# Leaving o out of the second half's sum and gates in an LSTM step, and forming it in later gaps

## The reference

```python
def step(carry, xw_t):                       # L0, 512 steps in sequence
    prev_h, prev_c = carry
    a = xw_t + prev_h @ Wh                   # Wh is 512 x 2048, order i, f, o, g
    i = sigmoid(a[:, :H]); f = sigmoid(a[:, H:2*H]); o = sigmoid(a[:, 2*H:3*H])
    g = tanh(a[:, 3*H:])
    next_c = f * prev_c + i * g
    next_h = o * tanh(next_c)
    return (next_h, next_c), next_h
x = x + lstm(x, cond, Wx, Wh, b)
x = x + ssm(x, cond, conv_b, Wp, bp, Ws, bs, A_log, dt_log, Wo, bo)   # convolution, projections, a linear scan
```

## Time and profile before

| | us |
|---|---|
| median of 3 runs | 1920.33 (1919.08 to 1920.81) |
| the profiled execution | 1920.7 |
| its span | 1918.8 |
| one step in mid-run | 3.57 (DVE's line 951 of half 0 at 1000.30 and 1003.87) |

### The profile page before, as it was taken

The page is one execution under the profiler, slowest core; times in us unless marked ns, Lnnn a source line. Parts: engine busy times, 40 slices in busy tenths (PEclk is TensorE's granted clock), DMA queues, the critical chain, the costliest instruction groups (busy, mean ns, idle before and its releaser), DMA issues.

```text
span 1918.8 us, 123325 instructions
## 1 busy us (share of the span) xinstructions
PE 1814.8 (95%) x52714; PEld 1422.2 (74%) x52714; DVE 1389.9 (72%) x6917; ACT 1015.4 (53%) x4055; POOL 340.0 (18%) x1544
## 2 busy tenths in 40 slices
PE   5888999999999999999999999999999999999976
PEld 3666777777777777777777777777777777777865
DVE  8676667777677776777777677777777777767675
ACT  5555455555555555555555545556555555545442
POOL 1111111111111111111111111111111111111110
PEclk9999999999999999999999999999999999999998
DMA  6111111111111211111111111211111111211100
GB/s 236 51 45 37 48 53 37 51 56 43 54 49 41 64 41 55 48 47 56 47 56 40 53 54 39 62 45 51 53 52 48 45 56 40 72 39 48 47 15 24
DMA packets 112668, 100.81 MB, mean 53 GB/s; under 512 B 20353, under 2 KB 86453, under 8 KB 111094
## 3 DMA queue, kind: packets, MB, share of 16 engines
q1 hardware_dynamic: 111704, 90.79, 15.5%
q10 hardware_dynamic: 416, 2.13, 0.3%
HBM read 50.90 MB, written 41.94 MB: 48 GB/s over the span
## 4 chain that ended last, share of the span: by engine, by line
PE 78%; DVE 10%; ACT 5%; issue 3%; POOL 2%; DMA 1%; SPq 0%; ACTq 0%; POOLq 0%; DVEq 0%
PE recA L546 28%; PE recB L553 23%; PE pw L505 12%; PE pbc L623 10%; DVE tr L937 4%; ACT act L819 3%; POOL h L472 2%; DVE hz L968 2%; DVE pre L943 2%; DVE prod L951 1%; ACT tc L829 1%; PE pw L489 1%; PE po L643 1%; PE pu L596 1%; DMA wpk<-in_L_cond_Wh_dram 1%
## 5 line engine op out<-in xcount | busy, mean ns | idle before, releaser
L819 ACT ACTIVATE act<-pre 128x64 f32<-128x64 f32 x1024 | 262.7, 257 | 858.3 <-DVE pre L946 841.0
L546 PE MATMUL recA<-whi,hz 128*16 128x256 f16 x8176 | 516.7, 275 | 74.8 <-DVE hz L968 63.1
L553 PE MATMUL recB<-whi,hz 128*32 128x128 f16 x16352 | 578.8, 219 | 1.1 <-issue 1.1
L553 PE MATMUL recB<-wlo,hz 128*32 128x128 f16 x16352 | 578.6, 219 | 0.0
L546 PE MATMUL recA<-wlo,hz 128*16 128x256 f16 x8176 | 513.3, 273 | 0.0
L553 PEld LDWEIGHTS recB<-whi,hz 128*32 128x32 f16 x16352 | 438.5, 97 | 11.3 <-issue 1.6
L553 PEld LDWEIGHTS recB<-wlo,hz 128*32 128x32 f16 x16352 | 438.3, 97 | 2.5
L546 PEld LDWEIGHTS recA<-whi,hz 128*16 128x16 f16 x8176 | 200.2, 88 | 304.1 <-DVE hz L968 281.3
L937 DVE STREAM_TRANSPOSE tr<-recA 128x256 f32<-128x256 f32 x512 | 229.9, 449 | 198.3 <-PE recA L546 196.3
L623 PE MATMUL pbc<-yt,wpk 128*128 128x256 f32 (+5 forms) x1120 | 329.5, 400 | 0.0
L472 POOL TENSOR_TENSOR h<-osc,tc 128x16 f32<-128x16 f32 x1024 | 228.1, 223 | 467.2 <-ACT tc L829 467.2
(11 more groups left out here) (164 smaller groups left out, 1993.0 us busy)
## 6 DMA issues: line engine op xcount, KB each, us to landing
xw_rows<-xs SPq DMA_DIRECT2D x128, 256.0 KB, 2.3
seed<-xw_rows SPq DMA_DIRECT2D x1008, 32.0 KB, 2.0
xn<-in_x_dram SPq DMA_DIRECT2D x32, 256.0 KB
out_dram<-ot SPq DMA_DIRECT2D x32, 256.0 KB, 3.1
seed<-in_L_cond_Wh_dram ACTq DMA_DIRECT2D x2, 1024.0 KB, 6.8
wpk<-in_L_cond_Wh_dram SPq DMA_DIRECT2D x2, 1024.0 KB, 12.0
wlo<-in_L_cond_Wx_dram SPq DMA_DIRECT2D x2, 1024.0 KB, 13.3
xs<-in_L_cond_Wx_dram SPq DMA_DIRECT2D x1, 1024.0 KB, 9.5
```

The costliest lines, as they stand in the source:

```text
L546: ins = pe.matmul(rec[0][32 * j:32 * j + 2 * NB, 0:256].rearrange("p (c f) -> p c f", c=2), h[:, 2 * NB:4 * NB], w[:, k, :, :].rearrange(" ...
L553: ins = pe.matmul(rec[1][32 * j:32 * j + 32, 0:128], h[:, 2 * NB * (1 - c):2 * NB * (1 - c) + 32], w[:, k, 4 * (2 + c) + j, :], start=Fals ...
L819: act_eng.activation(act[q][:, 0:G, :].rearrange("p g n -> p (g n)"), pre[q][:, :, :, :].rearrange("p g c b -> p (g c b)"), ACT.Tanh, scal ...
```

## The change

Half 1 no longer takes o through the same add and the same tanh as the other gates. Its transpose reads the two 64 column halves of recB in reverse order, so that the blocks lie as o, g, i, f in tr[1], pre[1] and act[1]. `add` and `gates` of half 1 work on rows 1 to 3 (48 elements). o's own sum is a new DVE instruction `add_o` between half 0's cell and half 1's product. o's tanh is a new ACT instruction `gate_o` in the place of `opened`. osc[1] = (o + 1) SC is formed on POOL instead of ACT, between POOL's two products. `product` reads its operands at the new places. Half 0 is as it was.

```diff
+        ifgate, gc = (act[0][:, 0:2, :], act[1][:, 2:4, :]), (act[0][:, 3:5, :], act[1][:, 1:5:3, :])
@@ gpsimd
                 pool.tensor_scalar(osc[0][:, :], act[0][:, 2, :], 1.0, SC, ALU.add, ALU.mult).then_inc(s_os[0], 1)
                 for q in range(2):
+                    if q:
+                        pool.wait_ge(s_tgo, t + 1)
+                        pool.tensor_scalar(osc[1][:, :], act[1][:, 0, :], 1.0, SC, ALU.add, ALU.mult).then_inc(s_os[1], 1)
                     pool.wait_ge(s_tc[q], t + 1)
                     pool.wait_ge(s_os[q], t + 1)
@@ scalar
             def gates(t, q):
                 act_eng.wait_ge(s_add[q], t + 1)
-                act_eng.activation(act[q][:, 0:G, :].rearrange("p g n -> p (g n)"),
-                                   pre[q][:, :, :, :].rearrange("p g c b -> p (g c b)"), ACT.Tanh, scale=gain).then_inc(s_tg[q], 1)
-
-            def opened(t):
-
-                act_eng.wait_ge(s_tg[1], t + 1)
-                act_eng.activation(osc[1][:, :], act[1][:, 2, :], ACT.Copy, bias=SC, scale=SC).then_inc(s_os[1], 1)
+                act_eng.activation(act[q][:, q:G, :].rearrange("p g n -> p (g n)"),
+                                   pre[q][:, q:G, :, :].rearrange("p g c b -> p (g c b)"), ACT.Tanh, scale=gain).then_inc(s_tg[q], 1)
+
+            def gate_o(t):
+                act_eng.wait_ge(s_addo, t + 1)
+                act_eng.activation(act[1][:, 0, :], pre[1][:, 0, :, :].rearrange("p c b -> p (c b)"), ACT.Tanh,
+                                   scale=gain).then_inc(s_tgo, 1)
@@ scalar, order of a step
                     tanh_c(t, 0)
-                    opened(t)
+                    gate_o(t)
@@ vector
             def open_(t, q):
                 dve.wait_ge(s_rec[q], t + 1)
-                order = ("p c g z b -> p (c g z b)", "p g c z b -> p (g c z b)")[q]
-                dve.transpose(tr[q][:, :, :, :, :].rearrange(order), rec[q][:, 0:WIDTH[q]]).then_inc(s_tr[q], 1)
+                if q:
+                    dve.transpose(tr[1][:, :, :, :, :].rearrange("p g c z b -> p (g c z b)"),
+                                  rec[1][:, 0:128].rearrange("p (a f) -> p a f", a=2)[:, ::-1, :]).then_inc(s_tr[1], 1)
+                else:
+                    dve.transpose(tr[0][:, :, :, :, :].rearrange("p c g z b -> p (c g z b)"), rec[0][:, 0:256]).then_inc(s_tr[0], 1)
             def add(t, q):
                 dve.wait_ge(s_tr[q], t + 1)
                 if q:
-                    dve.tensor_tensor(pre[1][:, :, :, :], tr[1][:, :, :, 0, :],
-                                      tr[1][:, :, :, 1, :], ALU.add).then_inc(s_add[1], 1)
+                    dve.tensor_tensor(pre[1][:, 1:G, :, :], tr[1][:, 1:G, :, 0, :],
+                                      tr[1][:, 1:G, :, 1, :], ALU.add).then_inc(s_add[1], 1)
+            def add_o(t):
+                dve.tensor_tensor(pre[1][:, 0, :, :], tr[1][:, 0, :, 0, :], tr[1][:, 0, :, 1, :],
+                                  ALU.add).then_inc(s_addo, 1)
             def product(t, q):
                 dve.wait_ge(s_tg[q], t + 1)
-                dve.scalar_tensor_tensor(prod[q][:, :, :], act[q][:, 0:2, :], 1.0, act[q][:, 3:5, :],
+                dve.scalar_tensor_tensor(prod[q][:, :, :], ifgate[q], 1.0, gc[q],
                                          ALU.add, ALU.mult).then_inc(s_prod[q], 1)
@@ vector, order of a step
                     add(t, 1)
                     cell(t, 0)
+                    add_o(t)
                     product(t, 1)
```

More of the change, by code:

```diff
@@ L140, in lstm_ssm_kernel @@
         s_tg = [sem(f"s_tg{q}") for q in range(2)]
+        s_addo, s_tgo = sem("s_addo"), sem("s_tgo")
         s_tc = [sem(f"s_tc{q}") for q in range(2)]
```

## The result

The changed kernel takes 1943.4 us (median of 4 runs, 1940.5 to 1948.24) against 1919.7 us (4 runs, 1918.29 to 1920.81) for the kernel before on the same chip: a ratio of 1.0125, 95% interval 1.0111 to 1.0139. It is slower by 24 us where 14 us less was forecast. The profiled execution took 1948.2 us with a span of 1946.3.

What follows compares the result with a forecast made beforehand. The prediction took half 1's chain in the recurrence loop to bound the kernel, not TensorE. 15 + 17 = 32 ns a step gave 14.3 us, from 1920.33 to 1906.0; forecast 1902 to 1911 (70%), range 1901 to 1917.

Steps and rivals of the forecast that it cites:

- What bounds the step: Recurrence loop ending in `low`: half 1's chain sets the step by about 0.02 us, half 0 right behind.
- The add: Half 1's add on DVE, 64 to 48 elements: 15 ns less, on the path of both chains.
- The gates: Half 1's gates on ScalarE, 64 to 48 elements: 17 ns less for half 1, about 12 ns for half 0.
- The sum: Whole run: 436 x 0.032 + 17 x 0.018 = 14.3 us gained.
- The reversed read: recB's transpose on DVE: price 0 taken, slack 0.01; as a slower rival up to 0.12 us longer, 1956, 5%.
- o's sum and tanh in their gaps: `add_o` in DVE's idle 0.24 us and `gate_o` in the copy's place on ScalarE: price 0 each.
- o + 1 on GpSimd: Third GpSimd instruction, 0.20 us, between the halves' products: price 0, slack 0.08 at the lower bound, none at the upper.
- my own upper bound: A 0.08 gap on GpSimd before o + 1, ending 1005.19, just when half 1's `high` wants it.
- The sign that I had named for being wrong: On DVE, `high` of half 1 waiting for GpSimd instead of its tanh would show the prediction wrong.
- GpSimd is late: Rival: gap before o + 1 above 0.08, each further 10 ns takes back 4.5 us; 1911 to 1919, 10%.
- The rival of the lock: Rival: o + 1 on GpSimd blocks half 0's `low` on DVE at SBUF, step 0.11 longer, 1970; 6%.
- TensorE's other work: Steps limited by TensorE's queue: 58 of 511 start late, about 17 gain partly, 436 have room for all.

Runs made afterwards that it cites:

- a_no_o: The changed kernel without half 1's o sum, tanh and o + 1, osc[1] being a constant written once; 1906.72 us, ratio 0.9928 to the kernel before.
- a_pool_tt: The changed kernel with half 1's o + 1 on GpSimd replaced by a tensor_tensor, o times o (wrong values); 1910.22 us, one execution, beside 1921.29 before.
- b_pool_early: The kernel before with half 1's o + 1 on GpSimd, its wait written first, ahead of GpSimd's first product; 1986.75 us, ratio 1.0339.
- a_swap: The changed kernel with the two waits before half 1's last product on DVE and GpSimd in the other order; 1941.89 us, ratio 1.0103 to before.

## Why the prediction was wrong, step by step

**What bounds the step: right.** `low` released recA in both kernels, half 1 was last, and half 0 right behind.

**The add: right.** 203 ns for 48 elements in the changed kernel (15 ns forecast, 16 measured). **The gates:** 14 ns instead of 17 in duration, and 13 in what holds half 0 (12 forecast):

```profile
L954 DVE TENSOR_TENSOR pre<-tr 128x48 f32<-128x48 f32 x512 | 103.7, 203 | 0.0
L826 ACT ACTIVATE act<-pre 128x48 f32<-128x48 f32 x512 | 124.4, 243 | 7.4 <-DVE pre L954 2.1
L945 DVE STREAM_TRANSPOSE tr<-recB 128x128 f32<-128x128 f32 x512 | 162.1, 317 | 37.7 <-PE recB L559 2.1
```

The 207 ns that I took for 16 elements were the mean of two cases: 199 in half 0, where the tanh stands behind the gates on ScalarE, and 216 in half 1, where it waits for its cell. From 216 to 257 the slope is 0.85 ns per element and gives the 14. The 0.833 ns per element of the Trainium skill ("ScalarE: Activation LUTs", section "What ACT_TABLE_LOAD costs") agrees: 13 ns. Both chains came out 0.029 sooner, 32 forecast for half 1.

**The sum: right for what it covered.** 14.3 us were forecast, and a_no_o, which has that part alone, gains 14.6. That the two are so close is partly luck: the interval is 10 to 18, and the step got 0.028 to 0.029 shorter, not 0.032.

**The reversed read: right.** The transpose of recB takes 317 ns as before and the add starts at 1.140 in both.

**o's sum and tanh in their gaps: right**, no cost that the runs can tell.

**o + 1 on GpSimd: wrong, and this step carries the result.** Two terms of it failed. First, "I take the lower end, as there is nothing left to wait for": the gap was 0.084, the upper end. POOL does not start a tensor_scalar behind another instruction without one. By my own upper bound this alone was to use up the slack and cost nothing more; it makes o + 1 end at 2.318, 0.012 after the tanh, which with the usual hand-over would have cost some 0.015 a step (an estimate from the two ends), 6 to 7 us of the gain. Second, the hand-over from o + 1 to `high` was put at 0.04, the one seen behind a wait that travels. The wait for o + 1 is the separate one, and behind that the runs show 0.10 on DVE and 0.15 on POOL, where POOL's usual hand-over is 0.08. So o + 1 would have had to be over 0.07 before the tanh, and it was over 0.012 after it; together that is the 0.083. Less the 0.029 gained it is 0.054 a step, and over 436 to 453 steps 24 us, the measured difference. The sign that I had named for being wrong, `high` of half 1 waiting for GpSimd instead of for its tanh, is what came. The rival "GpSimd is late" named the place and the point, 0.08, and its price of 4.5 us for each 10 ns holds (0.083 is 37 us, less the 14 gained); it began to count 0.07 too late and so ended at 1919.

**The rival of the lock: wrong at this distance, and not empty.** `low` of half 0 starts 0.034 after POOL's product has ended and takes 0.175 as before. In a_pool_tt it starts 0.08 into POOL's o + 1 and takes 0.175 too. Nor does POOL's o + 1, which starts 0.05 into `low` in the changed kernel, take longer (0.204, as o + 1 of half 0). At 0.02 apart b_pool_early shows 0.05 of hindrance. The Trainium skill's rule ("SBUF — State Buffer", section "Who interferes with whom") is that the second instruction blocks for the whole of the first. By this case's numbers something of the kind exists, but it is seen only within 0.05 us of the first one's start, costs 0.05 and not 0.2, and is absent for instructions of 16 elements that start 0.07 apart.

**TensorE's other work: about right.** 84 steps of the changed kernel start late by it instead of 58, as the loop up to half 0's `low` became shorter.

## What to carry to other kernels

Before an operation is moved to an idle engine, look whether it becomes the neighbour of another instruction there and whether those kinds overlap: on GpSimd the 0.35 us free between its two products were not the question, the 0.13 between two ways of starting was. Where an instruction has two waits, write the one that ends last first, so that it travels with the work, and count the other with its own, longer hand-over: 0.10 and not 0.03 on DVE. Two that end together can't both travel. Where the slack is a few hundredths, the 0.07 between the two hand-overs decides. That the price begins when the separate wait ends 0.07 before the other is worked out from the two hand-overs: in the runs it costs nothing at 0.09 before (`low` in every kernel), 0.058 at 0.012 before (a_swap) and 0.083 at 0.012 after, and no run lies between the first two.

## What the runs showed of the hardware

- GpSimd, 16 elements: tensor_tensor behind tensor_tensor starts 0.043 before the first has ended; a tensor_scalar has 0.063 to 0.084 of idle time on either side, with or without a wait, whether DVE is busy or idle.
- Of two waits the one written first travels with the work, and the other is an instruction of its own. Behind the end of what the separate one waits for the work starts after 0.10 instead of 0.03 on DVE, and on GpSimd after 0.135 to 0.15 instead of 0.08 (each also by exchanging the order). One that is over 0.09 or more before the other delays nothing.
- DVE's cell instruction (two SBUF inputs, 16 elements) takes 0.05 longer when it starts within 0.05 after a GpSimd product has started, and nothing more when it starts 0.07 after it.
- ScalarE writing 128 elements to PSUM held the engine for 0.29 us, where a tanh of 16 elements holds it for 0.11.
